# Decoder layer in float32: values weighted ahead of the decays' differences, a tap group split in two, GpSimd's gate chunks one product later, expert numbers written in place

## The chip, the cores and the metric

One Trainium2 chip, one core of it. The metric is the device time of one execution in microseconds (us), the median of several. Engines: TensorE (PE), VectorE (DVE), ScalarE (ACT), GpSimd (POOL), SyncE (SP, which issues most transfers).

## What is computed

One decoder layer on 8 batches of 512 tokens with 512 features, all float32:

```
x = layernorm(x + attn(x))              # decaying state + 5-tap convolution along the tokens
x = layernorm(x + mlstm(x, ctx, ctx))   # 8 heads, exponential gates, running maximum of the log decays
x = layernorm(x + moe(x))               # router over 32 experts, top 2, capacity 160, plus 16 small experts

attn:  s_t = a s_{t-1} + (1-a) x_t ;  y = S W^T + b + conv5(x) + cb
mlstm: ig, fg = linear(q, k, v); cs = cumsum(log_sigmoid(fg))
       log_D[s,t] = cs[s] - cs[t] + ig[t]  (t <= s);  D = exp(log_D - max_t log_D)
       C = (q k^T / 8) * D;  h = C / (max(|sum_t C|, exp(-max)) + 1e-6) v ;  layernorm(h) * scale
moe:   probs = softmax(gelu([x, stats(x)] r1^T + b) r2^T); best two experts of each token;
       each expert takes its 160 tokens of highest probability;
       out = weighted experts' outputs + 0.05 * gate * small experts
```

## The kernel before, in words

The kernel has three parts in a row: a pipeline over the 8 batches (attn, mlstm, router), a selection of each expert's tokens, and a loop over the 32 experts. The change touches the first only.

**The pipeline.** `run_pipeline` calls on every engine a function `step(n, ...)` for n = 0 to 9. In step n, batch n gets its retention (attn) and its gates and first half of mlstm, batch n-1 its heads (`values`, `head_out`), batch n-2 its norms and router, and VectorE prepares batch n+1: for each of four chunks c of 128 features a scan over 512 tokens (`state_scan`, line 1448) and four taps of the convolution (`taps`, line 1458; the fifth tap is ScalarE's `inputs`). In steps 0 and 1 this preparation is at other places of the step, earlier (`first`); in step 7 there is no next batch. Each engine runs its list in the order written; a `then_inc` raises a semaphore at an instruction's end and a `wait_ge` holds the engine until it is raised.

**Retention.** TensorE's `retention(n, tb)` (lines 664 and 666) multiplies the states and the convolution of batch n into bank `Wb`; it waits for the last tap of chunk 3 and stands at the start of step n. ScalarE copies the rows (`raw_rows`, line 1091), VectorE takes their statistics (`norm1_stats`, line 1465).

**The gates of batch n.** 8 heads on 8 partitions, 512 tokens long. VectorE's `gates_2`: running sum (1585), sum with the input gate (1588), running maximum ("max", 1590), and a difference ("neg", 1592). `gates_3` (VectorE 1596, ScalarE 1151) and `gates_4` (VectorE 1600, ScalarE 1155, 1156) split the maximum into three bf16 parts. GpSimd's `gate_chunks` takes two differences against the ends of the 128-token chunks: "toend" (2218) and "fromend" (2221); it begins with a wait for VectorE's "max". TensorE's `gate_columns` (708) transposes the gates and waits for "neg" and "toend"; ScalarE's `gates_5` copies and exponentiates them (1177, 1178, 1179: the last is "w", the weight of each value row). The decays between chunks go another way: ScalarE's `gates_f` exponentiates "fromend" (1162) and rounds it to bf16 (1164, "Fhi"); VectorE's `gates_f` takes the remainder (1607, "Fr"); ScalarE's `gates_g` rounds that (1168 "Fm", 1169 "Fmid"); VectorE's `gates_g` takes the last remainder (1612, "Flo").

**The states of batch n.** VectorE's `weigh_values` (1498, 128 x 1560) multiplies the values of three chunks by "w". TensorE's `state` first spreads two decays (718, waits for "w", "Flo" and "Fmid"), then waits for the weighted values and multiplies keys and values of three chunks (728). ScalarE copies the first state (`first_state`, 1201), VectorE makes the later two (`later_states`, 1511 and 1514), and retention of the next batch waits for the banks.

**The router.** VectorE's `softmax_2` and `top_two` finish the softmax of batch n-3 in step n, find the best two experts, cast their numbers to float (1673, into `ex2`), compare them with 0..31 (1677, 1678), store the masked probabilities ("save", 1683) and copy `ex2` into `e_all` (1686), the table of all tokens' experts that the selection reads.

**Order of VectorE in a step n of 2 to 6, around the change:** scan of chunk 2 (1448), `head_out(n-1, 2)` (ending in 1541), taps of chunk 2, `gates_f`, `weigh_values`, `gates_g`, scan and taps of chunk 3, `later_states`.

Of the kernel before, what the change touches and what calls it, by code (L numbers as in the profile page):

```python
# [28 lines left out]
TB = T // P  # L29
NT = NB * TB  # L30
TAPS, PAD = 5, 2
# [115 lines left out]
def decoder_kernel(nc, xT_d, kT_d, v_d, decay_d, WT_d, b_d, cw_d, cb_d, wi_d, wf_d, ib_d, fb_d, ln_d,  # L147
# [5 lines left out]
    with ctx:  # L153
# [35 lines left out]
        e_all = keep.take(NT, 2)  # L189
# [10 lines left out]
        room = Room(arena, ROOM)  # L200
# [78 lines left out]
        pr = room.take(TB, NE)  # L279
        top8 = room.take(TB, 8)  # L280
        at8 = room.take(TB, 8, dt=U32)
        ex2 = room.take(TB, 2)
        oh0 = room.take(TB, NE)
        oh1 = room.take(TB, NE)
        wsum = room.take(TB)
# [1130 lines left out]
        def _(dve):  # L1416
# [31 lines left out]
                dve.tensor_tensor_scan(st, a_dec[:, c:c + 1].to_broadcast([P, T]), st, 0.0,  # L1448
                                       ALU.mult, ALU.add).then_inc(re_v(f"scan{c}"), 1)

            def taps(b, c):

                row = cv[b.slot][:, c, :]
                dve.wait_ge(*re_a.at(f"cv{c}", b))
                for i, k in enumerate(k for k in range(TAPS) if k != PAD):
                    if i:
                        dve.wait_ge(*re_v.at(f"tap{i - 1}_{c}", b))
                    dve.scalar_tensor_tensor(row, xT[:, c, k:k + T], cw[:, c, k:k + 1], row,  # L1458
                                             ALU.mult, ALU.add).then_inc(re_v(f"tap{i}_{c}"), 1)
# [204 lines left out]
            def top_two(b):  # L1664
                for tb in range(TB):
                    m = dve.max(top8[:, tb, :], pr[:, tb, :])
                m.then_inc(so_v("top"), 1)
                dve.wait_ge(*so_v.at("top", b))
                for tb in range(TB):
                    m = dve.max_index(at8[:, tb, :], top8[:, tb, :], pr[:, tb, :])  # L1670
                m.then_inc(so_v("at"), 1)
                dve.wait_ge(*so_v.at("at", b))
                dve.tensor_copy(ex2, at8[:, :, 0:2]).then_inc(so_v("cast"), 1)
                dve.tensor_tensor(wsum, top8[:, :, 0], top8[:, :, 1], ALU.add)
                dve.wait_ge(*so_v.at("cast", b))
                io = iota_e.unsqueeze(1).to_broadcast([P, TB, NE])
                dve.tensor_tensor(oh0, io, ex2[:, :, 0:1].to_broadcast([P, TB, NE]), ALU.is_equal)
                dve.tensor_tensor(oh1, io, ex2[:, :, 1:2].to_broadcast([P, TB, NE]), ALU.is_equal).then_inc(so_v("oh"), 1)
                dve.wait_ge(*so_v.at("oh", b))
                dve.tensor_tensor(oh0, oh0, oh1, ALU.add).then_inc(so_v("ohs"), 1)  # L1680
                dve.wait_ge(*so_v.at("ohs", b))
                pair = (b - b.slot).line(NE // 2)
                dve.tensor_tensor(sc_all[:, b.slot * TB:(b.slot + 1) * TB, bass.ds(pair, NE)], oh0, pr, ALU.mult)\
                    .then_inc(so_v("save"), 1)
                dve.reciprocal(wsum, wsum).then_inc(so_v("rec2"), 1)
                dve.tensor_copy(tiles_of(e_all, b), ex2)
                dve.wait_ge(*so_v.at("rec2", b))
                dve.tensor_tensor(tiles_of(w_all, b), top8[:, :, 0:2], wsum.unsqueeze(2).to_broadcast([P, TB, 2]),
                                  ALU.mult).then_inc(so_v("w"), 1)
# [37 lines left out]
            def tiles_of(ap, b):  # L1727
                return ap.rearrange("p (n a) e -> p n a e", a=TB)[:, b.line(1)]
# [39 lines left out]
            def step(n, a, s, r, x1, x2):  # L1768

                if n.off >= NB:  # L1770
                    if n.off == NB:
                        last_values(n - 1, n - 2)
                    return
                if r:
                    norm2_stats(n - 2)
                    norm2_scaled(n - 2)
                    norm3_sum(n - 2)
                first = n.off <= 1
                if n.off == 0:
                    retained(n + 1, 0)  # L1780
                    for tb in range(TB):
                        norm1_stats(n, tb)
                    norm1(n)
                    retained(n + 1, 1)
                    retained(n + 1, 2)
                    retained(n + 1, 3)
                if a and s:
                    norm1_stats(n, 0)
                if n.off == 1:
                    retained(n + 1, 0)  # L1790
                if s:
                    scale_queries(n - 1, 0)
                if a and s:
                    norm1_stats(n, 1)
                if n.off == 1:
                    retained(n + 1, 1)
                if r:
                    norm3_stats(n - 2)
                if a and s:
                    norm1_stats(n, 2)  # L1800
                if n.off >= 3:
                    softmax_2(n - 3)
                    top_two(n - 3)
                if s:
                    weigh(n - 1, 1)
                if a and s:
                    norm1_stats(n, 3)
                    norm1(n)
                if s:
                    head_out(n - 1, 0)  # L1810
                    scale_queries(n - 1, 1)
                if r:
                    router_extreme(n - 2, 0)
                    router_extreme(n - 2, 1)
                    router_sparse(n - 2)
                    router_stats(n - 2)
                x1 = x1 and not first
                if x1:
                    state_scan(n + 1, 0)
                if s:  # L1820
                    weigh(n - 1, 2)
                    head_out(n - 1, 1)
                if n.off == 1:
                    retained(n + 1, 2)
                    state_scan(n + 1, 3)
                if x1:
                    taps(n + 1, 0)
                if n.off == NB - 1:
                    dve.wait_ge(*re_t.at(f"w{TB - 1}", n))
                    dve.wait_ge(*so_v.at("save", n - 3))  # L1830
                    dve.wait_ge(*cs_p.at("iota", b0))
                early_choices(n, 0, 1)
                if s:
                    scale_queries(n - 1, 2)
                    weigh(n - 1, 3)
                early_choices(n, 2, 7, 3, 4, 5, 8, 9, 10)
                if x1:
                    retained(n + 1, 1)
                if n.off == 1:
                    head_out(n - 1, 2)  # L1840
                if a:
                    gates_2(n)
                    gates_3(n)
                if s:
                    scale_queries(n - 1, 3)
                if a:
                    gates_4(n)
                if x1:
                    state_scan(n + 1, 2)
                if n.off > 1 and s:  # L1850
                    early_choices(n, 6, 11)
                    head_out(n - 1, 2)
                if n.off == 1:
                    taps(n + 1, 3)
                if x1:
                    taps(n + 1, 2)
                if n.off == NB - 1:
                    dve.wait_ge(*ga_t.at("gates", n))
                early_choices(n, 12, 13)
                if a:  # L1860
                    gates_f(n)
                    weigh_values(n)
                    gates_g(n)
                early_choices(n, 14, 15)
                if x1:
                    retained(n + 1, 3)
                if a:
                    later_states(n)
                if s:
                    head_out(n - 1, 3)  # L1870
                if r:
                    softmax_1(n - 2)
                if a:
                    weigh(n, 0)
# [257 lines left out]
        def _(pool):  # L2132
# [74 lines left out]

            def gate_chunks(b):

                pool.wait_ge(*ga_v.at("max", b))  # L2210
                pool.wait_ge(*ga_t.at("cols", b - 1))
                pool.wait_ge(*ga_v.at("Fr", b - 1))
                pool.wait_ge(*ro_p.at("l2", b - 2))
                pool.wait_ge(*n1_p.at("shift", b))
                m3 = g_m[0:NH].rearrange("p (a t) -> p a t", a=TB)
                gm3 = gm.rearrange("p (a t) -> p a t", a=TB)
                ends = m3[:, 0:TB - 1, P - 1:P].to_broadcast([NH, TB - 1, P])
                pool.tensor_tensor(gm3[64:64 + NH, 0:TB - 1], gm3[0:NH, 0:TB - 1], ends, ALU.subtract)\
                    .then_inc(ga_p("toend"), 1)
                pool.wait_ge(*ga_p.at("toend", b))  # L2220
                pool.tensor_tensor(g_rel[0:NH], m3[:, 1:], ends, ALU.subtract).then_inc(ga_p("fromend"), 1)
# [217 lines left out]
```

## Time and profile before

| | us |
|---|---|
| median of 3 runs | 1659.94 (1658.31 to 1662.73) |
| profiled execution, its own time | 1662.29 |
| its span | 1660.2 |
| TensorE busy | 1470.9 (89%) |
| VectorE busy | 941.7 (57%) |
| ScalarE busy | 489.1 (29%) |
| GpSimd busy | 310.0 (19%) |
| mean granted TensorE clock | 0.942 of full |

The span runs from the first to the last instruction of the profiled execution; busy times are shares of it. Busy time says little of which engine bounds a stage: for that the chain of waits is read, which goes back from the last instruction, at each point to what released it. In lists of instructions a row shows the start in us from the span's start, the duration in us, engine, line and operation, output and input with their shapes, and in brackets how long the engine was idle before and whom it waited for. The granted clock is 1.00 at 2.4 GHz and 0.50 at 1.2 GHz.

### The profile page before, as it was taken

The page shows a single profiled execution, that of the slowest core. Times are in us where ns is not written, and L with a number is a line of the kernel's source. Part 1 is how long each engine was busy: PE and PEld are TensorE (multiplying, and loading weights), DVE is VectorE, ACT ScalarE, POOL GpSimd, SP SyncE. Part 2 cuts the span into 40 slices and gives each one's busy share as a digit, 9 for nine tenths or more (in the row PEclk, how much of TensorE's full clock was granted, in tenths as well). Part 3 has the DMA queues.
Part 4 walks back from the last instruction along what each step waited for, and adds up shares of the span by engine and source line. Part 5 has one row for each costly group of instructions (what it writes and reads, how often), then busy time and mean ns, then how long its engine had stood idle before and what let it go on. Part 6 is the DMA issues. An engine that isn't in the chain of part 4 may idle for free.

```text
span 1660.2 us, 29325 instructions
## 1 busy us (share of the span) xinstructions
PE 1470.9 (89%) x10876; PEld 1129.5 (68%) x10912; DVE 941.7 (57%) x2786; ACT 489.1 (29%) x1155; POOL 310.0 (19%) x399
## 2 busy tenths in 40 slices
PE   5679998898989731799999999999999999999995
PEld 3355555555556411678888788887888878888783
DVE  8567999999998989432433324333243332433364
ACT  4556566675756443000101001010010100101023
POOL 4011111121212200112112121121211212112135
PEclk9689999999999855799999999999999999999998
DMA  6203213132130262077676776767767677676796
GB/s 176 72 19 103 77 64 91 46 112 71 52 102 1 102 254 88 17 285 274 224 294 230 284 274 225 292 229 286 272 224 293 229 287 271 225 293 229 284 343 199
DMA packets 92575, 311.03 MB, mean 187 GB/s; under 512 B 42838, under 2 KB 46940, under 8 KB 83164
## 3 DMA queue, kind: packets, MB, share of 16 engines
q1 hardware_dynamic: 79260, 287.87, 47.4%
q0 software_dynamic: 13248, 22.29, 5.9%
q8 instruction: 39, 0.64, 0.2%
q14 instruction: 28, 0.23, 0.0%
HBM read 273.18 MB, written 36.96 MB: 187 GB/s over the span
## 4 chain that ended last, share of the span: by engine, by line
PE 69%; DVE 19%; issue 5%; ACT 3%; DMA 2%; POOL 1%; SPq 1%; DVEq 0%; POOLq 0%; ACTq 0%
PE bank L1039 36%; PE banks L1053 14%; PE bank L664 6%; PE banks L1056 4%; DVE arena L1458 3%; DVE arena L1448 2%; DVE arena L1905 2%; PE bank L666 1%; PE banks L766 1%; DMA arena<-acc_rows 1%; DVE arena L1630 1%; DVE arena L1620 1%; PE banks L747 1%; DVE arena L1498 1%; DVE arena L1479 1%
## 5 line engine op out<-in xcount | busy, mean ns | idle before, releaser
L1393 ACT ACTIVATE arena<-bank 128x160 f32<-128x160 f32 x288 | 87.1, 303 | 870.9 <-PE bank L1039 869.0
L1039 PE MATMUL bank<-keep,arena 128*128 128x160 f32 x2304 | 320.0, 299 | 1.8 <-DVE arena L2109 1.8
L1039 PE MATMUL bank<-arena 128*128 128x160 f32 x2304 | 319.7, 301 | 0.9 <-issue 0.9
L1039 PEld LDWEIGHTS bank<-keep,arena 128*128 128x128 f32 x2304 | 315.4, 189 | 5.7 <-issue 3.2
L1039 PEld LDWEIGHTS bank<-arena 128*128 128x128 f32 x2304 | 315.9, 191 | 4.2 <-issue 4.2
L2109 DVE TENSOR_TENSOR arena<-arena,bank 128x160 f32<-128x160 f32 x256 | 82.1, 321 | 405.3 <-ACT arena L1393 352.8
L1053 PE MATMUL banks<-arena 128*128 128x512 f32 x576 | 252.4, 592 | 0.0
L2296 POOL DMA_INDIRECT acc_rows<-arena,keep x64 | 102.8, 1606 | 628.2 <-DVE arena L2054 612.0
L1053 PEld LDWEIGHTS banks<-arena 128*128 128x128 f32 x576 | 107.6, 190 | 122.5 <-issue 122.5
L2052 DVE TENSOR_SCALAR arena<-banks,keep 128x512 f32<-128x512 f32 x32 | 24.0, 750 | 187.4 <-PE banks L1056 185.6
L664 PE MATMUL bank<-arena 128*128 128x512 f32 x224 | 107.9, 626 | 5.5 <-DVE arena L1458 5.5
L1458 DVE SCALAR_TENSOR_TENSOR arena<-arena 128x512 f32<-128x512 f32 x128 | 96.8, 756 | 3.4
L664 PEld LDWEIGHTS bank<-arena 128*128 128x128 f32 x224 | 43.7, 200 | 55.1 <-issue 44.2
L2042 DVE STREAM_TRANSPOSE keep<-arena 32x128 f32<-32x128 f32 x256 | 77.5, 303 | 3.8
L1195 ACT ACTIVATE arena<-bank,arena 128x128 f32<-128x128 f32 x256 | 72.0, 373 | 19.0 <-PE bank L626 19.0
L1056 PEld LDWEIGHTS banks<-arena 128*32 128x32 f32 x2304 | 60.9, 110 | 24.3 <-issue 24.3
L2042 DVE STREAM_TRANSPOSE arena<-arena 32x128 f32<-32x128 f32 x240 | 72.5, 302 | 3.6
L2284 POOL DMA_INDIRECT arena<-x_rows,keep x64 | 64.2, 1003 | 36.4 <-POOL keep L2276 26.6
L1056 PE MATMUL banks<-arena 128*32 128x128 f32 x2304 | 69.5, 274 | 0.0
L766 PE MATMUL banks<-arena 128*128 128x96 f32 x512 | 63.1, 277 | 5.7 <-DVE arena L1541 5.7
L766 PEld LDWEIGHTS banks<-arena 128*128 128x128 f32 x512 | 60.4, 192 | 10.1 <-issue 10.1
L2276 POOL COPY keep<-keep 128x2 int32 (+1 forms) x64 | 29.3, 457 | 175.6 <-DVE keep L2013 96.9
(290 smaller groups left out, 1788.4 us busy)
## 6 DMA issues: line engine op xcount, KB each, us to landing
arena<-in_wup SPq DMA_DIRECT2D x32, 4096.0 KB, 12.4
arena<-in_wdn SPq DMA_DIRECT2D x32, 2048.0 KB
arena<-in_aup SPq DMA_DIRECT2D x32, 512.0 KB, 11.6
arena<-in_xT SPq DMA_DIRECT2D x32, 256.0 KB, 2.8
arena<-in_kT SPq DMA_DIRECT2D x8, 1024.0 KB, 5.6
arena<-in_v SPq DMA_DIRECT2D x32, 256.0 KB, 6.4
x_rows<-arena SPq DMA_DIRECT2D x8, 1024.0 KB, 4.4
acc_rows<-arena SPq DMA_DIRECT2D x8, 1024.0 KB, 6.8
```

What stands on the lines that cost most here:

```text
L664: pe.matmul(w[:, :], ST[b.slot][:, c, rows], WT[:, c, :], start=(c == 0), stop=False)
L766: pe.matmul(pv[:, r * T + tb * PVN:r * T + (tb + 1) * PVN], weights(b, j)[:, r * T + tb * P:r * T + (tb + 1) * P], va[b.slot][:, tb, h * V ...
L1039: m = pe.matmul(u[:, g * CAP:(g + 1) * CAP], w, xeT[e.slot][:, c, :], start=(c == 0), stop=(c == C - 1))
L1053: m = pe.matmul(Yb[0][:, :], hact[:, j, 0:P], w, start=(j == 0), stop=(j == J))
L1056: m = pe.matmul(Yb[1][CAP2 * c:CAP2 * (c + 1), 0:P], hact[:, j, P:CAP], w[:, c * P:(c + 1) * P], start=(j == 0), stop=(j == J))
L1195: m = act.activation(d[:, tb * P:(tb + 1) * P], w[:, tb * P:(tb + 1) * P], ACT.Exp, bias=gcol[b.slot][:, tb, h:h + 1])
L1393: act.activation(sg[k], Ub[k][:, 0:CAP], ACT.Silu).then_inc(up_a(f"silu{j}"), 1)
L1458: dve.scalar_tensor_tensor(row, xT[:, c, k:k + T], cw[:, c, k:k + 1], row, ALU.mult, ALU.add).then_inc(re_v(f"tap{i}_{c}"), 1)
L2042: dve.transpose(xeT[e.slot][out, :, rows], full[rows, :, out])
L2109: dve.tensor_tensor(hact[:, j, :], sg[k], u, ALU.mult).then_inc(up_v(f"mul{j}"), 1)
L2284: pool.indirect_dma_start(out=xg[e.slot][:, cols], out_offset=None, in_=rows, in_offset=bass.IndirectOffsetOnAxis(ap=idx_g[e.slot][:, k:k ...
L2296: pool.indirect_dma_start(out=rows, out_offset=bass.IndirectOffsetOnAxis(ap=idx_s[e.slot][:, k:k + 1], axis=0), in_=yy[e.slot][:, cols], i ...
```

## The change

```diff
@@ -279,7 +279,6 @@
         pr = room.take(TB, NE)
         top8 = room.take(TB, 8)
         at8 = room.take(TB, 8, dt=U32)
-        ex2 = room.take(TB, 2)
         oh0 = room.take(TB, NE)
         oh1 = room.take(TB, NE)
         wsum = room.take(TB)
@@ -1448,11 +1447,12 @@
                 dve.tensor_tensor_scan(st, a_dec[:, c:c + 1].to_broadcast([P, T]), st, 0.0,
                                        ALU.mult, ALU.add).then_inc(re_v(f"scan{c}"), 1)
 
-            def taps(b, c):
+            def taps(b, c, which=range(TAPS - 1)):
 
                 row = cv[b.slot][:, c, :]
                 dve.wait_ge(*re_a.at(f"cv{c}", b))
-                for i, k in enumerate(k for k in range(TAPS) if k != PAD):
+                for i in which:
+                    k = i if i < PAD else i + 1
                     if i:
                         dve.wait_ge(*re_v.at(f"tap{i - 1}_{c}", b))
                     dve.scalar_tensor_tensor(row, xT[:, c, k:k + T], cw[:, c, k:k + 1], row,
@@ -1670,6 +1670,7 @@
                     m = dve.max_index(at8[:, tb, :], top8[:, tb, :], pr[:, tb, :])
                 m.then_inc(so_v("at"), 1)
                 dve.wait_ge(*so_v.at("at", b))
+                ex2 = tiles_of(e_all, b)
                 dve.tensor_copy(ex2, at8[:, :, 0:2]).then_inc(so_v("cast"), 1)
                 dve.tensor_tensor(wsum, top8[:, :, 0], top8[:, :, 1], ALU.add)
                 dve.wait_ge(*so_v.at("cast", b))
@@ -1683,7 +1684,6 @@
                 dve.tensor_tensor(sc_all[:, b.slot * TB:(b.slot + 1) * TB, bass.ds(pair, NE)], oh0, pr, ALU.mult)\
                     .then_inc(so_v("save"), 1)
                 dve.reciprocal(wsum, wsum).then_inc(so_v("rec2"), 1)
-                dve.tensor_copy(tiles_of(e_all, b), ex2)
                 dve.wait_ge(*so_v.at("rec2", b))
                 dve.tensor_tensor(tiles_of(w_all, b), top8[:, :, 0:2], wsum.unsqueeze(2).to_broadcast([P, TB, 2]),
                                   ALU.mult).then_inc(so_v("w"), 1)
@@ -1852,16 +1852,19 @@
                     head_out(n - 1, 2)
                 if n.off == 1:
                     taps(n + 1, 3)
-                if x1:
-                    taps(n + 1, 2)
                 if n.off == NB - 1:
                     dve.wait_ge(*ga_t.at("gates", n))
                 early_choices(n, 12, 13)
                 if a:
+                    weigh_values(n)
                     gates_f(n)
-                    weigh_values(n)
+                if x1:
+                    taps(n + 1, 2, (0,))
+                if a:
                     gates_g(n)
                 early_choices(n, 14, 15)
+                if x1:
+                    taps(n + 1, 2, (1, 2, 3))
                 if x1:
                     retained(n + 1, 3)
                 if a:
@@ -2207,7 +2210,7 @@
 
             def gate_chunks(b):
 
-                pool.wait_ge(*ga_v.at("max", b))
+                pool.wait_ge(*ga_v.at("neg", b))
                 pool.wait_ge(*ga_t.at("cols", b - 1))
                 pool.wait_ge(*ga_v.at("Fr", b - 1))
                 pool.wait_ge(*ro_p.at("l2", b - 2))
```

Four edits:
- `top_two` writes the two expert numbers by its cast into this batch's part of `e_all` and reads them there; the buffer `ex2` and the copy behind "save" are gone.
- VectorE's `weigh_values(n)` stands ahead of `gates_f(n)` instead of between `gates_f(n)` and `gates_g(n)`, in all of steps 0 to 7.
- `taps` takes a list of taps. In steps 2 to 6 the first tap of chunk 2 is issued between `gates_f` and `gates_g`, the other three behind `gates_g`; all four stood ahead of `gates_f`. (In step 7 `early_choices`, preparations of the selection, stand between as before.)
- GpSimd's `gate_chunks` begins with a wait for "neg" instead of "max".

## Rows read from the trace of the kernel before

**Rows 1.** Page part 4: the chain of waits, share of the span by line

```profile
PE bank L1039 36%; PE banks L1053 14%; PE bank L664 6%; PE banks L1056 4%; DVE arena L1458 3%; DVE arena L1448 2%; DVE arena L1905 2%; PE bank L666 1%; PE banks L766 1%; DMA arena<-acc_rows 1%; DVE arena L1630 1%; DVE arena L1620 1%; PE banks L747 1%; DVE arena L1498 1%; DVE arena L1479 1%
```

**Rows 2.** Chain of waits in time: start us, us, what

```profile
293.75 2.28 DVE arena L1630
...
359.74 2.28 DVE arena L1630
...
426.75 2.28 DVE arena L1630
```

**Rows 3.** TensorE in time, last parts of steps 3 and 4

```profile
259.33 0.24 PE L718 MATMUL bank<-arena 72*128 72x2 bf16 x4 [1.69 <-DVE arena L1612]
...
263.54 5.40 PE L664 MATMUL bank<-arena 128*128 128x512 f32 x8 [1.89 <-DVE arena L1458]
...
330.60 3.71 PE L664 MATMUL bank<-arena 128*128 128x512 f32 x8 [0.46 <-DVE arena L1458]
```

**Rows 4.** VectorE in time, step 4

```profile
288.49 0.69 DVE L1465 BATCH_NORM_STATS2 arena<-arena 128x6 f32<-128x512 f32 x1 [1.99 <-ACT arena L1091]
```

**Rows 5.** Groups by line and shape: count, busy us, mean ns, idle

```profile
L1686 DVE COPY keep<-arena 128x8 f32<-128x8 f32 x8 | 1.1, 142 | 0.0
```

**Rows 6.** VectorE in time, step 3

```profile
247.49 0.68 DVE L1592 TENSOR_TENSOR arena<-arena 8x512 f32<-8x512 f32 x1
248.20 1.21 DVE L1596 TENSOR_TENSOR arena<-arena 8x512 f32<-8x512 f32 x1
...
250.10 0.68 DVE L1600 TENSOR_TENSOR arena<-arena 8x512 bf16<-8x512 bf16 x1 [0.23 <-ACT arena L1155]
250.82 1.23 DVE L1448 TENSOR_TENSOR_SCAN arena<-arena 128x512 f32<-128x512 f32 x1
...
252.78 0.69 DVE L1541 TENSOR_TENSOR arena<-banks,arena 128x512 f32<-128x512 f32 x1
...
256.41 0.54 DVE L1607 TENSOR_TENSOR arena<-arena 8x384 f32<-8x384 f32 x1
256.88 1.76 DVE L1498 TENSOR_TENSOR arena<-arena 128x1560 f32<-128x1560 f32 x1
258.67 0.55 DVE L1612 TENSOR_TENSOR arena<-arena 8x384 bf16<-8x384 f32 x1
...
260.40 3.09 DVE L1458 SCALAR_TENSOR_TENSOR arena<-arena 128x512 f32<-128x512 f32 x4
```

**Rows 7.** GpSimd in time, step 3

```profile
247.54 1.33 POOL L2218 TENSOR_TENSOR arena<-arena 8x384 f32<-8x384 f32 x1 [12.47 <-DVE arena L1590]
248.94 1.15 POOL L2221 TENSOR_TENSOR arena<-arena 8x384 f32<-8x384 f32 x1
```

**Rows 8.** GpSimd, line 2203: duration ns min/median/max, first and last start

```profile
L2203 POOL TENSOR_SCALAR arena<-arena x8: 232/1218/1221, 164.6 to 579.6; 128x4 f32<-128x4 f32 x8
```

**Rows 9.** ScalarE in time, step 3

```profile
253.51 0.19 ACT L1179 ACTIVATE arena<-bank 128x32 f32<-128x32 f32 x1
```

**Rows 10.** ScalarE in time, step 0

```profile
60.79 0.20 ACT L1177 ACTIVATE arena<-bank 128x32 f32<-128x32 f32 x1
```

**Rows 11.** TensorE in time, steps 0, 1 and 7

```profile
59.00 0.71 PE L708 MATMUL bank<-keep,arena 72*128 72x72 f32 x4 [9.22 <-DVE arena L1592]
...
66.48 0.25 PE L718 MATMUL bank<-arena 72*128 72x2 bf16 x4 [0.87 <-DVE arena L1612]
...
126.69 0.25 PE L718 MATMUL bank<-arena 72*128 72x2 bf16 x4 [0.88 <-DVE arena L1612]
...
523.06 0.25 PE L718 MATMUL bank<-arena 72*128 72x2 bf16 x4
```

**Rows 12.** Stretches: length, busy us by engine, granted clock, DMA

```profile
265.00:268.00 3.00, 3.00 (x5) 1.31 (x4) 2.83 (x9) 0.80 (x4) 0.00 (x0) 0.50 0.95 313
330.50:335.50 5.00, 4.60 (x16) 2.48 (x16) 4.72 (x14) 1.24 (x6) 0.00 (x0) 1.00 0.77 249
```

## The prediction

> **What bounds the kernel now.** I read the chain of waits first. By line it is mostly the experts' matmuls [rows 1], which start behind the router and hold none of the edited lines; what the change can move is the time at which the eight-batch pipeline hands over. Inside the pipeline I take the chain in order of time. One step repeats: the reduction L1630 stands on the chain at 293.75, 359.74 and 426.75 [rows 2], so a step lasts 65.99 or 67.01 us. From there to the last convolution tap VectorE is the chain, nearly without a pause; TensorE's retention L664 waits for that tap (idle 1.89 us, starts 263.54) [rows 3]; then TensorE and ScalarE lead until bn_stats L1465 takes over at 288.49 after VectorE idled 1.99 us [rows 4]. So in steps 2 to 6 (five of them) two things count: how long VectorE needs up to the last tap, and how fast retention runs after it. In steps 0 and 1 the taps were done early, and retention waits for the state matmuls L718/L728, thus for the gates. In step 7 there is no next batch.
>
> **Removed copy.** L1686 takes 0.14 us, eight times [rows 5]. In steps 3 to 7 it lies ahead of VectorE's 1.99 us pause for L1465, in the last three calls behind the `save` that the selection waits for. Saved on the path: 0, at most 8 x 0.14 = 1.1 us; the cast writes as many numbers as before, only elsewhere. If the pause before L1465 were gone, 0.1 us a step would show.
>
> **GpSimd one product later.** Now L2218 starts at 247.54, 0.05 us behind VectorE's L1592 (247.49), and takes 1.33 us; L1596 starts at 248.20 and takes 1.21; L2221 starts at 248.94 and takes 1.15 [rows 6, 7]. The subtraction L1607 with the same kinds of operands takes 0.54 for 384 columns and L1592 0.68 for 512, so L1596 is 0.53 too long. The ends fit an alternation in which each waits for the other: L1592 ends 248.17, L2218 0.70 later, L1596 0.53 after that, L2221 0.67 after that. A scan does the same to GpSimd: L2203, which in most steps is issued just behind a scan L1448 of 1.22 us, has a median of 1.218 us, and 0.232 at the shortest [rows 8].
>
> With the wait on `neg`, L2218 can start at about 248.24, while L1596 starts at 248.20 (0.03 us after L1592): VectorE is first. L1596 ends at 248.88 instead of 249.41, a gain of 0.53. L2218 then runs 248.88 to 249.58 beside scale_queries, which has one input in PSUM and was not stretched by GpSimd (beside L2221 it is no longer than elsewhere). ScalarE's m0 comes 0.53 earlier, L1600 starts at 249.56 and ends at 250.24 (now 250.78). But L2221 is due at 249.65 and has waited by then; it takes 250.24 to 250.91, and the scan L1448, now 250.82 to 252.05, starts 250.27 and is held to 250.91: of 1.22 us some 0.15 pass before operands are needed, so it ends at 251.98. Net gain per steady step: 0.06 us. The bounds: 0.6 if the scan isn't held, a loss of 0.1 if L2221 gets in ahead of L1600 as well.
>
> The Trainium skill speaks against this edit too: SBUF — State Buffer, section "Who interferes with whom", says that a VectorE instruction with both inputs in SBUF and a GpSimd instruction that reads SBUF exclude each other for the whole instruction, whoever issues first. By that rule the trace agrees at L1596 and L2203, and the stall is moved onto the scan; without it the edit would be worth 0.6 us a step.
>
> Who waits for GpSimd: gate_columns needs `toend`, now 248.87, then 249.58, while TensorE in a steady step is still in values 2 until about 250.1: covered by 0.5. The exponential of F needs `fromend` at 250.91 and runs after 253: covered by 2. In step 0 gate_columns starts at once, so it moves from 59.00 to 59.7, ends 60.4, and ScalarE's L1177, now 60.79 [rows 10], follows at 60.44 since m0 and mid are 0.53 earlier: gain 0.35 there.
>
> **Values ahead of the differences, taps split.** VectorE's sum of work stays. The order behind head_out 2 is now four taps, L1607 (256.41), L1498 (256.88, 1.76 long), L1612 (258.67), scan, four taps [rows 6]. L1498 needs ScalarE's L1179, ending 253.70 [rows 9]; with ScalarE 0.5 earlier (above) that is 253.2 and head_out 2 (L1541 from 252.78, less 0.06) ends at 253.41, so no stall; if ScalarE gains nothing, 0.3 us a step. Then: values to 255.09, L1607 to 255.55, first tap to 256.23, while ScalarE makes Fm (0.52) by 256.1: the one tap covers that wait. L1612 to 256.81, three taps to 259.18, scan to 260.3, four taps to 263.3 instead of 263.5: gain 0.17 with the 0.06 from above, the rest joints at which VectorE overlaps neighbours. Five steps: -0.85 us, bounds -3.7 (scan not held) and +1.5 (stall 0.3 each). The load of x for chunk 2 is let go 2.7 us later (after its last tap); its reader is a step away by some 15 us. SP has chunk 3 behind it, which still waits for the later tap.
>
> Steps 0 and 1: now L1607, then 1.76 of values, then L1612 gate L718. After: the values run in the wait for F, and L1607, Fm, L1612 take 0.54 + 0.54 + 0.56. In step 0 values would end at 64.0 (w 0.35 earlier), L1612 at 65.6 against 66.4: L718, now 66.48 after 0.87 of idle [rows 11], -0.8. In step 1 L1596 shorter by 0.53 lets TensorE's chain start earlier, but four taps, one of them held by L2221, end at 122.7; values to 124.4, L1612 to 126.0 against 126.6; L718 was at 126.69: -0.6. Step 7: L1612 ends 0.3 us later, but L718 runs at 523.06 with no idle ahead of it because TensorE is busy, 0.8 us behind L1612's end: 0, cover 0.5. Together -1.4, bounds -2.4 and 0.
>
> **TensorE's clock.** L1612 ends 1.9 us earlier in a steady step, so L718, which now waits 1.69 us for it, follows at once, and the state matmuls end at 259.3 instead of 261.6. The two pauses (1.69 before L718, 1.89 before L664) become one of about 4 us. What pauses do here: behind both the clock stood at 0.50 from 265 to 268 (1.2 instead of 2.4 GHz), and the L664 of 263.54 took 5.40; in the next step it was 1.00 from 330.5 on and L664 took 3.71 [rows 3, 12]. Of the five such groups three are of the first kind and two of the second. In the fast steps the fall came before, onto the state matmuls, where VectorE hides it. The price is the difference of the steps: 67.01 - 65.99 = 1.02 to 1.07. With no state matmuls in the middle of the pause, a fall must land on L664: I take all five slow, 2 x 1.07 = +2.1, and +1.0 for the fall lasting longer once (between 0 and, if all of L664 and L666 went at 1.2 GHz, 3.6 a step). Bounds of the term: -3.2 (no step slow) and +10.
>
> The Trainium skill, TensorE: Matmul & The Clock Gate, Part 1 (The HAM clock gate), says that the gate follows recent activity on a beat that doesn't start with the kernel. The trace agrees, with like pauses and unlike outcomes; no single run here can show the spread between executions.
>
> **The sum.** -0.85 - 1.4 + 0 + 3.1 = +0.9 us. Against the profiled execution's 1662.29 (span 1660.2 and 2.1 around it) that is 1663.2; that execution was 2.35 above the median, and the same 0.9 on 1659.94 gives 1660.8. The experts' stage moves as a block.
>
> **Rivals.**
> A. GpSimd's second product doesn't hold the scan, and the rest follows: -0.6 more in each of five steps and at the taps of step 1, some -3.5, time 1657.3. For it: no row shows which side wins when a waiting GpSimd meets back-to-back VectorE work in this place. Against: L2218 got in between L1592 and L1596, 0.03 us apart [rows 6, 7].
> B. TensorE's clock does no worse than now: -3.1, time 1657.7. With A, 1654.2, the only way to faster by over 0.3%.
> C. Slower: the one long pause makes retention run at 1.2 GHz for most of its first block. Place: L664 and L666 at the start of steps 3 to 7 of TensorE. Price up to 3.6 a step less what is in the sum; it decides once the five steps lose on average over 1.5 us more than now. Typical 5 x 1.9 = 9.5 - 2.2 = +7, time 1667. For it: nothing shows a pause of 4 us here, and the pauses of 1.7 to 1.9 already bring the low level. Against: the work behind the pause is dense, and the clock came back within the first group each time.
> D. The change doesn't do what it says: GpSimd still gets in ahead of L1596 (a race of 0.04 us). Then L1596 stays at 1.2, the scan is free, values stall 0.3: 5 x 0.2 and -0.7 for steps 0 and 1, with the clock 1663.4.
>
> **Chances.** Forecast 0.47, A 0.14, B 0.13, C 0.15, D 0.11. A measurement here tells 0.3% (5.0 us) from no change: faster means under 1655.0, slower over 1664.9. Faster comes from A and B together and the tails: 0.12. Slower is C and a tail of D and the forecast: 0.18. Same: 0.70. Range 1656 to 1665.5: low end A with half of B, high end a clock term of +8.
>
> **What would show it.** L1596 at 0.68 us in all eight; L2221 near 1.2 us; L1448 behind L1600 at about 1.7 us (at 1.22 rival A); L1498 right behind head_out 2 with no stall; L718 with no idle, one pause near 4 us before L664; step 0's L718 0.8 us earlier relative to L1585. The forecast is wrong if steps 2 to 6 differ by over 1 us each from now, or if L664 takes 3.7 us in most of them.

## The result, and the profile after

The change took 1664.5 us (median of 15, 1663.09 to 1667.6) beside 1660.99 us before (15 runs, 1657.72 to 1663.6): ratio 1.0023, 95% interval 1.0016 to 1.003, so 3.5 us more. A second comparison gave 1667.34 us beside 1660.11 us, ratio 1.0040 (1.0027 to 1.0053). The forecast was 1660.8 us with a range of 1656 to 1665.5, so the first comparison lies inside the range and the second 1.8 us above its upper end; the mechanism is the forecast's, the size of its clock term is not. One execution of one kernel below (the second of "filled and scan free") took 1840.42 us at a mean clock of 0.817 and is left out.

The profiled execution of the change has a span of 1662.4 us. Its chain by line is that of before, with more of it on retention (L663 was L664):

```profile
PE bank L1038 36%; PE banks L1052 14%; PE bank L663 7%; PE banks L1055 4%; DVE arena L1458 4%; DVE arena L1908 2%; PE bank L665 2%; DVE arena L1447 1%; PE banks L765 1%; PE bank L811 1%; DMA arena<-acc_rows 1%; DVE arena L1630 1%; DVE arena L1498 1%; DVE arena L1620 1%; DVE arena L1479 1%
```

The chain in time (start, us, what), the reductions that open each step's middle [rows 2]:

```profile
223.94 2.28 DVE arena L1630
...
291.78 2.28 DVE arena L1630
...
359.87 2.28 DVE arena L1630
...
428.02 2.28 DVE arena L1630
```

The steps last 67.84, 68.09 and 68.15 us, where 65.99 and 67.01 stood before.

VectorE in step 3 (start, us, engine, line, operation, output<-input, count), to be read against [rows 6]:

```profile
245.45 0.68 DVE L1596 TENSOR_TENSOR arena<-arena 8x512 f32<-8x512 f32 x1
...
246.82 0.68 DVE L1600 TENSOR_TENSOR arena<-arena 8x512 bf16<-8x512 bf16 x1 [0.23 <-ACT arena L1154]
247.54 1.74 DVE L1447 TENSOR_TENSOR_SCAN arena<-arena 128x512 f32<-128x512 f32 x1
...
250.62 1.77 DVE L1498 TENSOR_TENSOR arena<-arena 128x1560 f32<-128x1560 f32 x1
252.31 0.54 DVE L1607 TENSOR_TENSOR arena<-arena 8x384 f32<-8x384 f32 x1
252.77 0.73 DVE L1458 SCALAR_TENSOR_TENSOR arena<-arena 128x512 f32<-128x512 f32 x1
253.54 0.55 DVE L1612 TENSOR_TENSOR arena<-arena 8x384 bf16<-8x384 f32 x1
...
257.50 3.09 DVE L1458 SCALAR_TENSOR_TENSOR arena<-arena 128x512 f32<-128x512 f32 x4
```

L1596 is at 0.68 us instead of 1.21, the scan behind L1600 at 1.74 instead of 1.23. The values start 0.08 us ahead of head_out's end, with no stall; L1612 waits for nothing but the tap ahead of it. GpSimd in the same stretch [rows 7]:

```profile
245.49 1.33 POOL L2221 TENSOR_TENSOR arena<-arena 8x384 f32<-8x384 f32 x1 [13.17 <-DVE arena L1592]
246.90 1.29 POOL L2224 TENSOR_TENSOR arena<-arena 8x384 f32<-8x384 f32 x1
```

Now TensorE: the state's L717 once, and the first group of retention in each of the five steps, 3 to 7 of TensorE [rows 3]:

```profile
193.78 5.40 PE L663 MATMUL bank<-arena 128*128 128x512 f32 x8 [4.02 <-DVE arena L1458]
...
254.29 0.25 PE L717 MATMUL bank<-arena 72*128 72x2 bf16 x4
...
260.64 6.37 PE L663 MATMUL bank<-arena 128*128 128x512 f32 x8 [4.01 <-DVE arena L1458]
...
328.48 6.59 PE L663 MATMUL bank<-arena 128*128 128x512 f32 x8 [4.01 <-DVE arena L1458]
...
396.57 6.67 PE L663 MATMUL bank<-arena 128*128 128x512 f32 x8 [4.02 <-DVE arena L1458]
...
464.71 6.74 PE L663 MATMUL bank<-arena 128*128 128x512 f32 x8 [4.01 <-DVE arena L1458]
```

L717 has no idle before it (it had 1.69 us), and each retention comes after one pause of 4.0 us. The groups take 5.40, 6.37, 6.59, 6.67 and 6.74 us; before, they took 5.49, 5.40, 3.71, 5.40 and 3.71. The granted clock around the second of them (the last three columns are clock, DMA share, GB/s) [rows 12]:

```profile
258.00:260.00 2.00, 0.00 (x0) 0.00 (x0) 1.89 (x4) 0.00 (x0) 0.00 (x0) 0.81 0.16 62
...
264.00:266.00 2.00, 2.00 (x4) 0.75 (x3) 2.00 (x4) 1.70 (x6) 0.00 (x0) 0.50 0.88 320
266.00:268.00 2.00, 2.00 (x13) 1.39 (x12) 1.97 (x7) 0.95 (x2) 0.00 (x0) 0.99 1.18 273
```

The level falls within the pause, before retention begins, and is back only after 266. So it is in the last four of the five steps; in the first it falls inside the group (mean 0.69 from 194 to 195).

In steps 0, 1 and 7 the start of L717 (L718 in [rows 11]):

```profile
64.69 0.25 PE L717 MATMUL bank<-arena 72*128 72x2 bf16 x4 [0.48 <-DVE arena L1612]
...
124.07 0.25 PE L717 MATMUL bank<-arena 72*128 72x2 bf16 x4 [0.77 <-DVE arena L1612]
...
526.57 0.25 PE L717 MATMUL bank<-arena 72*128 72x2 bf16 x4
```

To compare kernels without what lies ahead and behind, I use the time from the first to the last start of the gates' scan L1585 (steps 0 to 7): before, then after.

```profile
L1585 DVE TENSOR_TENSOR_SCAN arena<-arena x8: 1210/1211/1212, 54.3 to 508.8; 8x512 f32<-8x512 f32 x8
```

```profile
L1585 DVE TENSOR_TENSOR_SCAN arena<-arena x8: 1211/1212/1214, 53.2 to 512.3; 8x512 f32<-8x512 f32 x8
```

That is 454.5 us and 459.1 us, +4.6 us. The span grew by 2.2 only. The first scan came 1.1 us earlier, which no edit explains: over the kernels below it lies anywhere from 53.1 to 54.5. From the last scan to the last batch's router (L852, after L851) the change took 0.5 us more, and from there to the experts' L1039 (L1038) 1.9 us less, because in the profile before L852 ran slowly. It stands there at 3.68 us, against 1.98 in the profile after:

```profile
585.64 3.68 PE L852 MATMUL banks<-arena 128*128 128x512 f32 x4 [0.68 <-ACT arena L1242]
```

This place differs between executions of one kernel too (see the last pair of experiments).

### The profile page after: what moved, and what is told of

It is laid out like the page before. It is cut to its first block, busy times and chain, and to the rows that moved or that the text cites. A ratio compares the mean times of both kernels' runs of the same rounds, so it can differ in the third digit from the quotient of the medians.

```text
span 1662.4 us, 29322 instructions
## 1 busy us (share of the span) xinstructions
PE 1472.5 (89%) x10876; PEld 1129.4 (68%) x10912; DVE 940.2 (57%) x2778; ACT 489.7 (29%) x1155; POOL 311.7 (19%) x399
## 4 chain that ended last, share of the span: by engine, by line
PE 70%; DVE 18%; issue 5%; ACT 3%; DMA 2%; POOL 1%; SPq 1%; DVEq 0%; POOLq 0%; ACTq 0%
PE bank L1038 36%; PE banks L1052 14%; PE bank L663 7%; PE banks L1055 4%; DVE arena L1458 4%; DVE arena L1908 2%; PE bank L665 2%; DVE arena L1447 1%; PE banks L765 1%; PE bank L811 1%; DMA arena<-acc_rows 1%; DVE arena L1630 1%; DVE arena L1498 1%; DVE arena L1620 1%; DVE arena L1479 1%
## 5 line engine op out<-in xcount | busy, mean ns | idle before, releaser
L1038 PE MATMUL bank<-keep,arena 128*128 128x160 f32 x2304 | 320.0, 299 | 2.2 <-DVE arena L2112 2.2
L1038 PE MATMUL bank<-arena 128*128 128x160 f32 x2304 | 319.3, 301 | 0.9 <-issue 0.9
L1038 PEld LDWEIGHTS bank<-keep,arena 128*128 128x128 f32 x2304 | 315.4, 189 | 6.0 <-issue 3.2
L1038 PEld LDWEIGHTS bank<-arena 128*128 128x128 f32 x2304 | 315.4, 191 | 4.2 <-issue 4.2
L663 PE MATMUL bank<-arena 128*128 128x512 f32 x224 | 116.2, 666 | 20.1 <-DVE arena L1458 20.1
L663 PEld LDWEIGHTS bank<-arena 128*128 128x128 f32 x224 | 46.6, 214 | 73.9 <-issue 49.3
```

The lines of the kernel that those rows point to most:

```text
L663: pe.matmul(w[:, :], ST[b.slot][:, c, rows], WT[:, c, :], start=(c == 0), stop=False)
L1038: m = pe.matmul(u[:, g * CAP:(g + 1) * CAP], w, xeT[e.slot][:, c, :], start=(c == 0), stop=(c == C - 1))
```

## The experiments

Each kernel is one or two edits away from before or from the change; times are medians, and ratios are to the kernel before run beside them (medians 1661.22, 1662.13, 1659.35 and 1660.11 us), so kernels of different groups are better compared by ratio. "Way of VectorE" is from L1630's start on the chain to the start of the following retention, step 4 to 5 (before 293.75 to 330.60, 36.85 us; after 291.78 to 328.48, 36.70 us); in "before, matmuls added" it ends with the added matmuls and not with VectorE's last tap.

| kernel | us | ratio (95%) | way of VectorE | L1585 first to last |
|---|---|---|---|---|
| before | 1660.99 | 1 | 36.85 | 454.5 |
| the change | 1664.5 | 1.0023 (1.0016 to 1.003) | 36.70 | 459.1 |
| GpSimd's wait alone | 1660.42 | 0.9994 (0.9985 to 1.0002) | 36.82 | 453.5 |
| order alone | 1668.65 | 1.0038 (1.0025 to 1.0051) | 37.09 | 460.6 |
| change, pause filled | 1654.96 | 0.9964 (0.9952 to 0.9977) | 36.71 | 449.3 |
| change, two pauses | 1661.03 | 0.9993 (0.9984 to 1.0002) | 36.71 | 453.6 |
| change, scan free | 1667.71 | 1.0032 (1.002 to 1.0045) | 36.73 | 459.6 |
| before, matmuls added | 1668.13 | 1.0039 (1.0026 to 1.0052) | 39.86 | 462.2 |
| filled and scan free | 1654.57 | 0.9961 (0.9948 to 0.9974) | 36.72 | 448.0 |
| order at the ends alone | 1657.85 | 0.9977 (0.9968 to 0.9985) | 36.83 | 451.3 |
| change, pause half filled | 1658.15 | 0.9994 (0.9985 to 1.0003) | 36.70 | 451.2 |
| change, copy put back | 1667.66 | 1.0044 (1.0032 to 1.0056) | 36.71 | 459.6 |
| the change, again | 1667.34 | 1.0040 (1.0027 to 1.0053) | 36.70 | 459.0 |
| copy put back, again | 1667.32 | 1.0039 (1.0026 to 1.0052) | 36.70 | 460.1 |

**GpSimd's wait alone.**

```diff
-                pool.wait_ge(*ga_v.at("max", b))
+                pool.wait_ge(*ga_v.at("neg", b))
```

> The kernel before with one edit of the change: GpSimd's gate chunks wait for neg instead of max. Theory 1 (the loss is TensorE's clock, brought down by one pause of 4 us in place of two of 1.7 and 1.9 us): the two pauses stay, L1596 falls to 0.68 us, the scan behind L1600 grows to 1.74 us, VectorE's way through a step changes by under 0.1 us, L664 stays at 3.7 or 5.4 us; time within 1.5 us of before (1661.0), a little below it. Theory 2 (the loss is the stall that GpSimd's second product puts on VectorE's scan): the time is that of the change, 1664.5.

As expected of theory 1. VectorE in step 3:

```profile
246.55 0.68 DVE L1596 TENSOR_TENSOR arena<-arena 8x512 f32<-8x512 f32 x1
...
247.92 0.68 DVE L1600 TENSOR_TENSOR arena<-arena 8x512 bf16<-8x512 bf16 x1 [0.23 <-ACT arena L1155]
248.64 1.73 DVE L1448 TENSOR_TENSOR_SCAN arena<-arena 128x512 f32<-128x512 f32 x1
```

Both lengths of the change are here, 0.53 us gained and 0.51 lost, and the time is that of before. So the stall on the scan is real and is not what the change lost.

**Order alone.** The change with `pool.wait_ge(*ga_v.at("max", b))` as before.

> The change without its edit on GpSimd (gate chunks wait for max again); the values ahead, the taps split, no copy. Theory 1: the pause of about 4 us before L663 is there, L663 takes 6.4 to 6.7 us in most of the five steps, and the values wait 0.3 us for ScalarE's L1178: 1664.5 to 1666. Theory 2: the scan is back at 1.22 us and the time at that of before or up to 1.5 us above, 1661 to 1662.5.

```profile
249.95 1.23 DVE L1447 TENSOR_TENSOR_SCAN arena<-arena 128x512 f32<-128x512 f32 x1
...
252.87 1.78 DVE L1498 TENSOR_TENSOR arena<-arena 128x1560 f32<-128x1560 f32 x1 [0.27 <-ACT arena L1178]
```

The scan is back at 1.23 us and the values wait 0.27 us for ScalarE, as forecast for that case; the first retention groups take 6.34 to 6.39 us behind pauses of 3.97 us. The time is 2.6 us above my upper end; in its profile the last router's L851 took 3.36 us, where the change's first profile had 1.98. It refutes theory 2: the scan unstalled, the time far above before. It also shows what GpSimd's wait is worth in the new order: the way of VectorE is 0.39 us shorter with it, five times.

**Change, pause filled.**

```diff
+                w = Wb[tb % 2]
+                if tb == 0 and b.off >= 3:
+                    pe.wait_ge(*st_a.at("S0", b - 1))
+                    for _ in range(16):
+                        pe.matmul(w[:, :], identh, upper_h.rearrange("p a t -> p (a t)"), start=True, stop=True)
                 pe.wait_ge(*re_v.at(f"tap{TAPS - 2}_{C - 1}", b))
-                w = Wb[tb % 2]
```

> The change, with 16 extra bf16 matmuls of 512 columns (some 3.5 us at 2.4 GHz) into retention's free bank ahead of its wait for the last tap, from batch 3 on; their result is overwritten. Theory 1: TensorE is busy through the pause, the clock stays at 1.00, L663 takes 3.4 to 3.8 us, a step takes about 65.9 us (now 67.8 to 68.1), 1654 to 1657. Theory 2: nothing on VectorE changes, so the time stays at 1664.5 or above it if the extra matmuls are late for retention.

TensorE in step 3: the added matmuls, retention, and what follows it. Then its granted clock:

```profile
256.02 3.62 PE L657 MATMUL bank<-arena 128*128 128x512 bf16 x16
260.22 3.71 PE L667 MATMUL bank<-arena 128*128 128x512 f32 x8 [0.59 <-DVE arena L1462]
...
265.27 0.39 PE L624 MATMUL bank<-arena 128*128 128x512 bf16 x1 [0.46 <-ACT arena L1198]
```

```profile
260.00:264.00 4.00, 3.78 (x11) 1.85 (x12) 3.73 (x13) 0.12 (x1) 0.00 (x0) 1.00 0.63 180
```

The matmuls compute nothing that is used. VectorE's way is the same to 0.01 us, all five groups take 3.71 us, the steps last 65.8 to 65.9 us, and the kernel is 9.5 us below the change's 1664.5 (L1585 first to last: 9.8). The idle 0.46 us at 265.27 is ScalarE's, the floor that made a fast group worth 1.07 us and not 1.7.

**Change, two pauses.**

```diff
             def state(b):
+                if 2 <= b.off < NB - 1:
+                    pe.wait_ge(*re_v.at(f"tap{TAPS - 2}_2", b + 1))
                 pe.wait_ge(*ga_a.at("w", b))
```

> The change, with TensorE's state matmuls (L717, L727) held in steps 2 to 6 until the last tap of chunk 2 on VectorE, which puts them back into the middle of the pause, about 4.2 us ahead of retention as before. VectorE's list is that of the change. Theory 1: two pauses again, L663 takes 3.4 to 5.4 us, 1659.5 to 1661.5. Theory 2, and any theory in which VectorE's order costs the time: 1664.5, since only TensorE's idle time moved.

```profile
257.83 0.26 PE L719 MATMUL bank<-arena 72*128 72x2 bf16 x4 [2.05 <-DVE arena L1460]
...
261.97 3.71 PE L663 MATMUL bank<-arena 128*128 128x512 f32 x8 [1.79 <-DVE arena L1460]
...
327.79 5.78 PE L663 MATMUL bank<-arena 128*128 128x512 f32 x8 [1.22 <-DVE arena L1460]
```

A wait was added and nothing else, and the loss is gone: pauses of 2.05 and 1.79 us (in the slow steps 2.05 and 1.14 to 1.24, as the level had fallen while the state matmuls ran), five groups at 5.72, 3.71, 5.78, 3.71 and 5.78 us, the time that of before. In the two fast steps the granted clock stayed at 1.00 throughout. With the run above this is the cause, shown from both sides: filling the pause and splitting it both remove the loss while VectorE's list stands still.

**Change, scan free.**

```diff
                 pool.wait_ge(*ga_p.at("toend", b))
+                if 2 <= b.off < NB - 1:
+                    pool.wait_ge(*re_v.at("scan2", b + 1))
                 pool.tensor_tensor(g_rel[0:NH], ...
```

> The change, with GpSimd's second product held in steps 2 to 6 until VectorE's scan of chunk 2 has ended, so that it meets head_out's instructions that read PSUM. If the two exclude each other (theory 1's reading of the 1.74 us), the scan is back at 1.22 us, the product takes 0.7 us instead of 1.29, and VectorE's way from L1630 to retention is 36.2 us instead of 36.70. The pause before retention shrinks to about 3.5 us and still brings the clock down: gain 0.5 us in each of five steps less what the clock takes, 1660 to 1664. Rival: the scan is long for another reason (its data), then nothing changes, 1664.5.

VectorE, then GpSimd:

```profile
248.44 1.23 DVE L1447 TENSOR_TENSOR_SCAN arena<-arena 128x512 f32<-128x512 f32 x1
...
249.96 0.70 DVE L1536 TENSOR_SCALAR arena<-arena 128x8 f32<-128x8 f32 x1
```

```profile
249.81 0.81 POOL L2226 TENSOR_TENSOR arena<-arena 8x384 f32<-8x384 f32 x1 [2.08 <-DVE arena L1447]
```

The scan is at 1.23 us, so its 1.74 was GpSimd's. But I expected 36.2 us of VectorE's way and got 36.73: the stall moved on to L1536, a tensor_scalar of 128 x 8 that takes 0.70 us instead of 0.17. I had counted on instructions with one input in SBUF being free of GpSimd, and this one, in place in SBUF, is not. The time missed both expectations, 3 us above: L663 is as in the change (5.40 to 6.71 us), and in the last batch's router L851 and L858 took 3.20 and 3.62 us, see the last pair.

**Before, matmuls added.** The same 16 matmuls in the kernel before.

> The kernel before with the same 16 extra matmuls ahead of retention from batch 3 on. They start 1.9 us before the last tap is done and run 3.5 us, so they end 1.7 us after it: if their cost is their own time, L664 starts 1.7 us late but at the full clock and takes 3.7 us, and each slow step loses 0.6, each fast one 1.7: 1664 to 1667. Rival: the matmuls were good for something else than the clock in the run on the change (for instance they keep the weights' loads going), then 1655 here too.

```profile
262.28 0.63 PE L626 MATMUL bank<-arena 128*128 128x512 bf16 x1
262.70 4.19 PE L658 MATMUL bank<-arena 128*128 128x512 bf16 x16
266.73 3.60 PE L668 MATMUL bank<-arena 128*128 128x512 f32 x8
```

They start behind the state matmuls' second bank and hold retention to 266.73, 3 us after the last tap. Retention runs at the full clock and the kernel still loses 6 us to the one run beside it (1662.13), 1.1 more than my upper end. So the matmuls, 4.2 us long here, don't help in a pause of 1.9 us, and the rival, that they do something else useful, is refuted. I had their start 0.9 us too early, as the state matmuls themselves ran partly at the low level.

**Filled and scan free.** Both edits on the change.

> The change with both: the 16 extra matmuls in the pause and GpSimd's second product behind the scan. Clock and port both freed: VectorE's way from L1630 to retention 36.2 us at L663 3.7 us, a step 65.3 us, 0.5 us in each of five steps below the run with the matmuls alone: 1652.5, 1650.5 to 1654. If the extra matmuls end too late for the earlier tap, 1654 to 1656.

0.9961 against 0.9964: no difference that this measurement tells, and the expected 1650.5 to 1654 is missed. The expected 0.5 us a step rested on the same wrong point as above, L1536.

**Order at the ends alone.**

```diff
                 if a:
-                    gates_f(n)
-                    weigh_values(n)
+                    if 2 <= n.off < NB - 1:
+                        gates_f(n)
+                        weigh_values(n)
+                    else:
+                        weigh_values(n)
+                        gates_f(n)
                     gates_g(n)
```

on the kernel with GpSimd's wait alone, so with the old order of the taps.

> The kernel before with GpSimd's wait on neg, and the values ahead of the differences in steps 0, 1 and 7 alone; steps 2 to 6 keep their order and so their two pauses. Against the run with the GpSimd wait alone (1660.4) it gains 0.3 us in step 0 and 0.3 to 0.6 in step 1, nothing in step 7: 1659.6, 1658.5 to 1661. If what the change loses came from the order in the first and last steps, this would be over 1662.

1657.85 us, under the expected range: 0.0017 below the kernel with the wait alone by the ratios, 2.8 us, of which steps 0 and 1 were to bring 0.6 to 0.9. The retention groups were 3.71, 4.56, 5.58, 3.71 and 5.56 us in its profile against 5.57, 3.71, 5.56, 5.40 and 3.71, 0.8 us less in sum. By the starts of L1585 steps 0 and 1 were 0.5 and 1.0 us shorter than with the wait alone, not 0.6 to 0.9 together. The profiles of the two also differ in the last router, L852 at 1.98 us against 3.68, by 2.0 us up to the experts' L1039; as that place changes from one execution to the next (last pair), how much of the 2.8 us is the order's is not shown.

**Change, pause half filled.** The same with `range(8)`.

> The change with 8 extra bf16 matmuls of 512 columns (1.8 us) instead of 16, right behind the state matmuls, from batch 3 on: the pause before retention is about 2.3 us instead of 4.0 or 0.6. If what counts is how long TensorE is idle in one piece, L663 takes 3.7 us in some steps and 4 to 5.6 us in the others: 1656 to 1660, between the runs with 16 and with none. If only full cover helps, 1663 to 1665.

```profile
260.64 3.71 PE L667 MATMUL bank<-arena 128*128 128x512 f32 x8 [2.30 <-DVE arena L1462]
...
326.45 5.40 PE L667 MATMUL bank<-arena 128*128 128x512 f32 x8 [2.29 <-DVE arena L1462]
```

Pauses of 2.3 us, two groups at 5.40 and three at 3.71, where the kernel before had three slow and two fast; in the three fast steps the granted clock stayed at 1.00. The effect goes with the length of the pause: 0.6 us none of five slow, 2.3 us two of five, at 5.40; 4.0 us all five, at up to 6.75. These runs change the whole idle time and its longest piece together; the run with two pauses (3.8 us in two pieces, three of five slow) is the one that changes the pieces alone.

**Change, copy put back**, and the pair that it made necessary:

> The change with ex2 and its copy put back; the other three edits stay. My reading: the copy lies ahead of a pause of VectorE or behind save, so it costs nothing: 1664.5, 1663.5 to 1665.5. Rival: eight copies of 0.14 us are on the path, or the cast into the other buffer was what paid, then 1665.6 or more.

The time missed my range by 2.2 us on the rival's side, while its five retention groups agreed with the change's to 0.1 us and L1585 first to last to 0.5. Most of the difference was in the last batch's router, where its clock fell and the change's hadn't. So both ran once more, side by side:

> The change itself, once more, on the same chip as the next run. In its first profile TensorE's clock stayed at 1.00 in the last batch's router (L851, 1.98 us, L858, 1.97 us). If that is this kernel's rule, the time is 1664.5 again and the profile shows the same; if the fall there is chance from one execution to the next, some executions lie 2.5 to 3 us higher, and a second profile may show it.

> The change with ex2 and its copy put back, once more. Its first profile had every group of the five steps within 0.1 us of the change's, and a fall of the clock in the last batch's router (L852, 3.19 us, L859, 3.62 us) that the change's profile hadn't. If the copy (0.14 us on VectorE, off the chain) tips the clock there as a rule, it is again 2 to 3 us above the run beside it; if it was chance, the two are within 1 us of each other.

1667.34 and 1667.32 us, ratios 1.0040 (1.0027 to 1.0053) and 1.0039 (1.0026 to 1.0052): no cost of the copy can be told (each ratio is good to 0.0013, 2 us). TensorE in the last router, first profile of the change, then its second:

```profile
589.68 1.98 PE L851 MATMUL banks<-arena 128*128 128x512 f32 x4 [0.68 <-ACT arena L1241]
592.57 1.97 PE L858 MATMUL banks<-arena 128*128 128x32 f32 x16 [0.91 <-ACT arena L1247]
```

```profile
589.42 3.20 PE L851 MATMUL banks<-arena 128*128 128x512 f32 x4 [0.68 <-ACT arena L1241]
593.39 3.62 PE L858 MATMUL banks<-arena 128*128 128x32 f32 x16 [0.78 <-ACT arena L1247]
```

The same kernel, 1.98 and 1.97 us in one execution, 3.20 and 3.62 in the other: here the clock differs from one execution to the next, by some 2.7 us of span. The two comparisons of the change are 0.17% apart, which is of that size; with one profile of each it is not shown that this is the reason. The change costs 0.2 to 0.4%.

## Why the prediction was right, and where its size was off

**Right: GpSimd one product later.** L1596 at 0.68 us in all eight, the scan at 1.74 where 1.7 was said, L2224 (L2221 before) at 1.29 where 1.2 was said. The net, 36.85 to 36.82 us with that edit alone, was said to be 0.06. Rival A fell, rival D too.

**Right: the order.** Way of VectorE 0.15 us shorter, 0.17 said. Without the help of GpSimd's wait the values stall 0.27 us, 0.3 said. From L1585 to the state's first matmul: step 0 from 54.33 to 66.48, then 53.24 to 64.69, 0.70 us less (0.8 said); step 1 from 113.09 to 126.69, then 111.09 to 124.07, 0.62 less (0.6 said). Step 7: nothing, as said; TensorE is busy until L717.

**Right as far as can be told: the copy.** 0 was said, and the pair side by side shows none within 2 us.

**Mis-sized: the clock.** The step of the prediction that failed is its last term, +3.1 us: "I take all five slow, 2 x 1.07", with +1.0 for one fall lasting longer. The profile gives for the five groups 31.77 us against 23.71, 8.1 us more. Of that, 0.6 us is slack in each of the two that were fast: a slow group before took 1.69 us longer, yet the matmul behind it and L666 (L625) came only 1.08 later, 6.13 us after the group's start instead of 5.05, since in a fast step it waits for ScalarE. That leaves 6.9 us. Added up, -0.7 -0.6 -5 x 0.15 + 6.9 = 4.8, and L1585 first to last says 4.6. All five slow was right; that a slow group costs as much as before was wrong. The edges of the low stretch around one retention, in the kernel before (start 263.54) and after (260.64), in the columns of the stretches above:

```profile
264.00:265.00 1.00, 1.00 (x4) 0.40 (x3) 0.93 (x3) 0.00 (x0) 0.00 (x0) 0.94 0.37 86
...
268.00:269.00 1.00, 1.00 (x4) 0.41 (x3) 1.00 (x3) 1.00 (x4) 0.00 (x0) 0.85 0.87 325
```

```profile
259.00:260.00 1.00, 0.00 (x0) 0.00 (x0) 0.93 (x3) 0.00 (x0) 0.00 (x0) 0.61 0.00 0
...
266.00:267.00 1.00, 1.00 (x5) 0.52 (x4) 1.00 (x3) 0.95 (x2) 0.00 (x0) 0.97 1.19 319
```

Before, the level falls at the end of the slice 264 to 265 and is back early in 268 to 269: some 3.4 us, all in the group, which loses half of that, 1.7. After, it falls in 259 to 260, 1.2 us ahead of the group, and is back as 266 begins: some 6.8 us, of which 5.4 lie in the group, and it loses 2.7. The prediction had this as a bound (3.6 us a step) and as rival C, and gave to the middle the price of the rows at hand, though these were of another kind of pause. The long stretch was in the kernel before as well, once, and the prediction did not read it: from 193.2 to 200.0, begun while the state matmuls ran, so that only its last 3.6 us fell on the group of 5.49.

Why the groups grow from 6.37 to 6.74 us can be read too. The last of them starts at 464.71:

```profile
464.00:465.00 1.00, 0.29 (x1) 0.29 (x2) 0.99 (x2) 0.00 (x0) 0.00 (x0) 0.51 1.31 212
...
470.00:471.00 1.00, 1.00 (x3) 0.48 (x2) 1.00 (x3) 0.00 (x0) 0.00 (x0) 0.57 0.08 16
```

The low stretch is again some 6.8 us, from 464.0 to 470.9. In the four steps it begins 1.2, 1.0, 0.8 and 0.7 us ahead of the group, so ever more of it falls on retention. In the first step it lasts some 3.4 us and lies wholly in the group, which takes 5.40.

**Between forecast and rival C.** Retention ran at the low level for most of its first group in four of the five steps, which is rival C's picture, while the price, steps 2 to 6 longer by 1.2 us on average, stayed under the 1.5 at which C was to decide. By the forecast's own sign of being wrong, "over 1 us each", it is at the edge: taken from one L1585 to the next, steps 2 to 6 changed by -0.3, +0.8, +2.1, +1.1 and +2.2 us.

**Luck.** The terms as measured add up to 4.8 us and not to 0.9. That the first comparison shows 3.5 us, inside the range, goes in its profiles with the earlier first scan (1.1 us) and the router's clock (1.9 us), which no term spoke of; the second comparison, 1667.34 us, is outside.

What remains open: why a low stretch lasts 3.4 us in one step and 6.8 in another, and what sets its start. The kernel alone does not: with the copy put back the first group took 5.40 us in one profile and 6.73 in the other, where all five took 6.67 to 6.75.

## What to carry to other kernels

When an edit lets a waiting engine run earlier, ask what its idle time will look like afterwards: here work worth nothing on the chain was moved out of the middle of TensorE's idle time, and the clock charged some 7 us for it. A low-priority batch of matmuls in the middle of a pause is worth keeping, and one wait that holds it there, or matmuls that fill all but 0.6 us of the pause, pays it back (1661.0 and 1655.0 us). Moving a GpSimd instruction out from behind one VectorE instruction put it behind the next here, twice; count the stall at its new place before counting the gain.

## What the runs showed of the hardware that was not expected

- A waiting GpSimd instruction gets in between two VectorE instructions 0.03 to 0.04 us apart, and not only those with two inputs wait for it: L1536, a tensor_scalar in place with one input, took 0.70 us instead of 0.17. The Trainium skill, SBUF — State Buffer, section "Who interferes with whom", counts tensor_scalar among the operations that can enter a mode with both ports, and so contend with GpSimd. The row agrees that it contends, no row shows the mode, and I had left that out.
- A pause of 4.0 us, with TensorE busy before and after, brought the low level in all five steps and in every profile; one of 2.3 us in two of five; one of 0.6 us in none. Two pauses of 1.69 and 1.89 us before the change (0.40 to 1.89 for the second) brought it in all five, but on the state matmuls and not on retention in two of them; two of 2.05 and 1.79 us in three of five.
- The fastest versions here are the change with the pause filled, 1654.96 us, 0.9964 (0.9952 to 0.9977) of before, and the same with the scan free, 0.9961, which the measurement does not tell apart. The version with the new order in the first and last steps alone, with GpSimd's wait, stands at 0.9977 without any added matmul (0.9968 to 0.9985).
